# Attention: the row maxima kept in the rounded f32 type and turned by a product with an identity of that type

## The reference

```python
x = x + diff_attention(layernorm(x))      # two causal softmaxes per head, 8 heads of 2 x 16
x = x + experts_gelu(layernorm(x))        # shared MLP and top 2 of 8 experts
x = x + causal_attention(layernorm(x))    # 16 heads of 8
x = x + experts_gelu(layernorm(x))
x = x + single_head_attention(layernorm(x))
x = x + full_attention_and_experts(x)     # rmsnorm, 16 heads of 8, no mask; then top 2 of 8 experts, swiglu
x = x + gated_recurrence(x)
x = x + full_attention_and_experts(x)
```

```python
scores = einsum('bhqd,bhkd->bhqk', q, k) * scale     # masked in the causal ones
attn = softmax(scores, axis=-1)
out = einsum('bhqk,bhkd->bhqd', attn, v)
```

## Time and profile before

| | |
|---|---|
| time, median of 3 runs | 2595.62 us (2595.09 to 2595.83) |
| the profiled execution | 2601.83 us, span 2600.1 us |
| TensorE busy / weight loads | 2246.4 us (86%) / 1646.6 us (63%) |
| VectorE, ScalarE, GpSimd busy | 1761.2, 1597.1, 1179.9 us |
| mean granted TensorE clock | 0.94 |
| turning the maxima (L1687) | 520 products in 260 calls |

### The profile page before, as it was taken

One profiled execution on the slowest core, in us unless ns is written; L12 is line 12 of the kernel. 1 busy time (PEld: TensorE's weight loads), 2 busy tenths in 40 slices (PEclk: granted clock), 3 DMA queues, 4 the chain that ended last, 5 costly groups with the idle time before them and its releaser, 6 DMA issues. The chain is left out here.

```text
span 2600.1 us, 59924 instructions
## 1 busy us (share of the span) xinstructions
PE 2246.4 (86%) x19192; PEld 1646.6 (63%) x19192; DVE 1761.2 (68%) x4845; ACT 1597.1 (61%) x3559; POOL 1179.9 (45%) x1645
## 2 busy tenths in 40 slices
PE   5999998899699888999778888889676788887896
PEld 3666665699566655799665555589333455555695
DVE  5677777444478776543767888576777577887666
ACT  3666665367566665476548888444465368887344
POOL 3456665445244555455122354457333323454463
PEclk9999999899799998999879999899888989999998
DMA  8000000322200002122100000222200000001225
GB/s 312 24 4 12 12 12 12 99 60 71 81 2 6 16 17 87 44 70 77 47 5 2 10 17 17 74 66 83 76 0 7 4 2 3 17 17 35 75 81 137
DMA packets 133603, 116.54 MB, mean 45 GB/s; under 512 B 22903, under 2 KB 119685, under 8 KB 131264
## 3 DMA queue, kind: packets, MB, share of 16 engines
q1 hardware_dynamic: 116032, 78.17, 10.4%
q0 software_dynamic: 17280, 34.65, 4.1%
HBM read 58.22 MB, written 56.36 MB: 44 GB/s over the span
## 5 line engine op out<-in xcount | busy, mean ns | idle before, releaser
L1216 ACT ACTIVATE A_Pm<-A_t 128x768 f32<-128x768 f32 (+1 forms) x512 | 469.1, 916 | 152.3 <-PE A_t L1645 149.5
L372 POOL DMA_INDIRECT ybuf<-F_yo,F_idx x284 | 315.7, 1112 | 265.0 <-DVE F_yo L581 161.2
L1412 DVE TENSOR_REDUCE A_padm<-A_s 128x4 f32<-128x1024 f32 x264 | 322.6, 1222 | 55.9 <-PE A_s L1637 53.2
L224 POOL DMA_INDIRECT xbuf<-xs,dst x256 | 268.4, 1048 | 105.9 <-issue 60.4
L733 PE MATMUL F_hb<-F_xT,F_wt 128*128 128x128 f32 x2272 | 311.3, 281 | 3.0 <-issue 1.5
L1672 PE MATMUL A_ot<-A_Pm,A_V 128*32 128x256 f32 (+3 forms) x3640 | 295.5, 389 | 16.9 <-POOL A_Pm L1111 10.0
L1645 PE MATMUL A_t<-A_Q,A_K 32*128 32x256 f32 (+1 forms) x2560 | 304.9, 332 | 0.0
L1111 POOL TENSOR_SCALAR_AFFINE_SELECT A_Pm<-A_Pm 128x512 f32<-128x512 f32 x256 | 168.4, 658 | 292.7 <-ACT A_Pm L1216 291.0
L733 PEld LDWEIGHTS F_hb<-F_xT,F_wt 128*128 128x128 f32 x2272 | 281.0, 195 | 9.4 <-issue 3.2
L1637 PE MATMUL A_s<-A_K,A_Q 32*128 32x256 f32 (+1 forms) x1584 | 202.7, 332 | 66.3 <-DVE A_padm L1412 31.3
L745 PE MATMUL F_out<-F_WA,F_g 128*128 x1704 | 247.9, 282 | 4.7 <-DVE F_g L572 1.6
(11 more groups left out here) (426 smaller groups left out, 5064.9 us busy)
## 6 DMA issues: line engine op xcount, KB each, us to landing
F_xr<-xbuf SPq DMA_DIRECT2D x284, 68.0 KB, 1.8
xbuf<-A_zero SPq DMA_DIRECT2D x16, 1088.0 KB, 17.5
xs<-ybuf SPq DMA_DIRECT2D x32, 512.0 KB, 6.9
ybuf<-F_yo,F_idx POOLq DMA_INDIRECT x284
xbuf<-xs,dst POOLq DMA_INDIRECT x256, 2.4
F_WA<-in_L_ffn_ew SPq DMA_DIRECT2D x2, 2048.0 KB, 9.0
F_WA<-in_L_ffn_ew SPq DMA_DIRECT2D x16, 256.0 KB, 5.8
F_WA<-in_L_ffn_e_gate SPq DMA_DIRECT2D x2, 1024.0 KB, 5.7
```

Source lines behind the costliest of these rows:

```text
L224: pool.indirect_dma_start(out=G["XBUF"][:, :], out_offset=bass.IndirectOffsetOnAxis(ap=G["dst"][:, t, c:c + 1], axis=0), in_=G["xs"][c][:, ...
L372: pool.indirect_dma_start(out=YBUF[:, :], out_offset=bass.IndirectOffsetOnAxis(ap=idx[n][:, h:h + 1], axis=0), in_=yo[r][:, h, :], in_offs ...
L1216: act.activation(Pm[r][:, j:j + 2, :], tbank[:, :].rearrange("p (j k) -> p j k", j=2)[:, :, 0:PW], ACT.Exp, scale=SCALE).then_inc(t_free, 1)
L1412: last = dve.reduce_max(tops.rearrange("p t j -> p j t"), sbank[:, :].rearrange("p (j t k) -> p j t k", j=2, t=TPS), AX)
```

## The change

`padm` becomes F32R (its memsets write the same zeros), a copy `identr` of the identity in F32R is made once by VectorE in `init_globals`, and `turn_max` issues a plain product of `padm` with `identr` where it issued a transpose of `padm` with `ident`. Every instruction keeps its place on its engine; one cast is added on VectorE ahead of the first stage.

```diff
@@ sparse_constants
     G["Mrun"] = ctx.enter_context(nc.sbuf_tensor("Mrun", [P, E], BF16))
+    G["identr"] = ctx.enter_context(nc.sbuf_tensor("identr", [P, P], F32R))
@@ init_globals, vector
                 dve.tensor_copy(xs[c][:, :, D], C["ids"][:, c, :])
+            dve.tensor_copy(G["identr"][:, :], ident[:, :])
@@ attention_stage
-    padm = [sb(f"padm{k}", [P, TPS, QUAD, GR]) for k in range(2)]
+    padm = [sb(f"padm{k}", [P, TPS, QUAD, GR], F32R) for k in range(2)]
@@ attention_stage, gpsimd
-            pool.memset(padm[0][:, :, :, :], 0.0)
-            pool.memset(padm[1][:, :, :, :], 0.0).then_inc(p_set, 1)
+            pool.memset(padm[0][:, :, :, :].bitcast(F32), 0.0)
+            pool.memset(padm[1][:, :, :, :].bitcast(F32), 0.0).then_inc(p_set, 1)
@@ turn_max
                 for t in range(TPS):
-                    last = pe.transpose(mbank[:, t * P:(t + 1) * P], padm[r][:, t, :, :].rearrange("p r g -> p (r g)"), ident[:, :])
+                    last = pe.matmul(mbank[:, t * P:(t + 1) * P], padm[r][:, t, :, :].rearrange("p r g -> p (r g)"), G["identr"][:, :], start=True, stop=True)
                 last.then_inc(mt_full, 1)
```

## The result

The changed kernel takes **2604.45 us** (median of 20 executions, 2598.43 to 2610.64); the kernel before took 2596.95 us (20 executions, 2593.12 to 2603.27) on the same chip. The ratio is 1.0025, with a 95% interval of 1.0018 to 1.0031: **slower by 0.25%**. The forecast of 2594.9 us was wrong, and so was its range, which ended at 2601. The profiled execution took 2604.19 us (span 2602.5), which is at the median; that of before was 4.9 us over its own. So the two profiles are only 2.4 us apart and show too little of the loss; it must be read by stage.

A forecast was written before the change was run, and what follows sets the result against it. TensorE was taken as the bound in the first attention stage (421 of 429 us busy), with slack elsewhere. Terms 0.3 - 0.5 - 0.8 + 0.3 = -0.7 us took the median from 2595.62 to 2594.9 us; range 2588 to 2601 us.

The forecast's parts named there:

- The pair: Two turned products at the changed line: 0.45 us to the end, 0.38 to the next load, taken as +0.005 us each.
- Behind the logits: Pairs after the router's logits: next load at 0.37 us instead of 0.46; -0.5 us first stage, -0.8 us other stages.
- The second load waits: Rival: the pair's second load starts only after the first product's columns, 0.054 us a pair, +6.3 to +14.0 us; chance 0.06.
- the load is as short: Rival: the rounded load is as short as the transposed one, saving 0.11 us a pair, 2583 to 2588 us; chance 0.04.
- the rounded maxima cost VectorE: Rival: writing maxima in the rounded type costs 9 ns or more at 792 reductions, up to +7 us; chance 0.03.
- the 177 pairs of the other stages: Pairs outside the first stage, not behind logits: only 0.005 us at each of 52 VectorE waits counts, +0.3 us.
- The clock (slower): Rival: less TensorE streaming lowers its clock; 13 us more at the lower level loses 5.2 us, 2602 us; chance 0.03.
- The clock (faster): Rival: plain products release the clock earlier in the last three attention stages, up to 4.8 us each, 2580.5 at best; chance 0.05.

The follow-up runs named there:

- e2: Changed kernel with f32 transposes instead of products, keeping the rounded type, identity copy and cast; 0.9980 of the kernel before.
- e10: Repeat, in a later comparison, of the changed kernel with f32 transposes and the rounded type kept; 1.0001 of the kernel before.
- e6: Changed kernel with the product only in the two unmasked stages (fourth and fifth), f32 transposes in the masked ones; 1.0018 of the kernel before.
- e9: The changed kernel unaltered, run again in a later comparison; 1.0031 of the kernel before.
- e1: The changed kernel unaltered, run again in another comparison; 1.0020 of the kernel before.
- e11: Changed kernel with both products of each pair streaming 256 columns, the second half into an unread block; 1.0019 of the kernel before.
- e5: Changed kernel with the product only in the two masked stages, f32 transposes in the unmasked ones, all types kept; 1.0002 of the kernel before.
- e4: Kernel before plus two unused f32 identity products after the third group's turn in the second, fourth and fifth stage; 1.0007 of the kernel before.

## Why the prediction was wrong

- **The pair: right.** 0.44 us to its end and 0.37 to the next load, forecast within 0.01; the longer load and the shorter streaming cancel. Behind the logits 0.37 instead of 0.46, as the sum had it. "The second load waits", "the load is as short" and "the rounded maxima cost VectorE" did not happen: the loads are 189 ns, the reductions 1222 ns as before, and e2 and e10 clear the type. The first stage shows it in one number, 304.96 against 305.01 us over 48 pairs.
- **The step that failed** is the sum's entry for the 177 pairs of the other stages: "TensorE has slack behind them", and of the pair "Only the 0.005 us in the result counts". I took slack as free for time saved on TensorE. It is free for time on the path; but the saving of 0.108 us in each group came out of what the array streams, in stretches of which some 40% held no product at all, and the clock then fell after some of them. The entry was worth +0.3 us in the sum; the fourth and fifth stage lost 5.2 us in the first profile, 12.4 to 14.7 in e6 and e9.
- **The rival that happened** is "The clock (slower)", named and priced, with a chance of 0.03. The price of a us was good: "5.2 us would be lost after 13 us more at it", and the profile has 5.2 us for 13.6 us. That the length came out near 13 us too is luck: nothing in the prediction said how much longer the clock would be low, and later profiles have 30.6 and 40.8 us. The reason against it was poor: "the upper level held through the rest of the stage with 15% of TensorE's time idle" is a mean over 311 us. The stage's sparsest stretches have 1.95 us of products in 3.40, 43% without any, and are found by cutting the stage into short stretches. In the trace of before they stood open, one at 1453.30, with the clock at 1.00 and nothing to tell how near to a fall it was.
- **Size.** The rows give 0.30 to 0.38 us lost for each us at the lower level (e1 against e2 9.0 us for 30.6, e9 against e10 14.7 for 40.8, e6 against e5 12.4 for 34.0, the first comparison 5.2 for 13.6). The other executions agree roughly by their mean clock: e9's 0.9343 against e10's 0.9390 is 0.0047 x 2 x 2655 = 25 us more at half rate, which at 0.30 to 0.38 is an estimate of 7.5 to 9.5 us, and the medians are 9.8 us apart. The profile of e9 shows more than that because it is its slowest execution. In the first comparison only the changed kernel's profile and before's can be set side by side; of its 7.5 us, 5.2 are shown in them and the rest is not placed. The range was also tighter than its own sum: the bounds reached +6.8 us, which is 2602.4, and the range was said to end at 2601. The measured time lies over both.
- **"The clock (faster)"** did not happen. The stretches of the earlier trace rows are as they were, with the first eight turned products in 22.00 us at 0.71 and the next eight in 17.20 at 1.00. The Trainium skill's page TensorE: Matmul & The Clock Gate (Part 4: PE-mode transpose) says that transposes don't count as the array being busy in the same way as products; with them replaced by plain products the clock should then have held better. It held worse: 3, 6 and 9 falls with the products (the changed kernel, e1, e9) against none with f32 transposes (before, e2, e10), and none either with plain products of the transposes' streaming length (e11). So for these f32 transposes of 128 columns the measurement speaks against the page.
- **A page that pointed near it.** The idle times that frame the fall are waits for VectorE and ScalarE of 0.7 us each. The Trainium skill's page TensorE: Matmul & The Clock Gate (section A second HAM failure mode: psum-queue depth-cycling) tells of another kernel, where TensorE idles briefly between groups of products often enough for its clock to go back and forth, and throughput suffers by it while the median product looks healthy. The falls here look like that, and I had not weighed it. But the same idle times stand in the kernel before, whose clock held, so the page doesn't tell the two kernels apart.
- The advice against the change (the Trainium skill, Perfetto Trace Analysis, section Transposes: turn by a transpose) held in its outcome, by a mechanism that the page doesn't name: at this size the transpose costs the pair the same time, and keeps the array streaming twice as long.

## What to carry to other kernels

TensorE's clock follows its own work, so time saved on it in a stage with slack need not be worth zero: here it was worth less. Before shortening TensorE's work in a stage with slack, cut that stage into stretches of a few us, find the sparsest, and ask what the edit takes out of it; a mean over the stage hides it, and busy time by records can't see columns. Where such an edit is wanted, try it first where the engine is the bound (here the product in the masked stages alone, e5, neither gained nor lost: 1.0002, and no fall in the others), and when a result is in, compare the granted clock of each stage before anything else. One profile shows one execution; the mean clock over all of them says whether it is typical.

## What the hardware showed that I had not expected

- The same 30 records in the same 2.06 of 3.40 us were followed by 1.00 of the clock or by 0.50; the work differed by 0.108 us of streaming, and the changed kernel too kept the upper level after most stretches like it. In all seven profiles with products in the full stages of which one or both streamed 128 columns there was a fall (1 to 9); of the seven with transposes there, or with both products 256 wide, six had none, and e4 had four.
- Idle time that stands together is not enough for a fall: e2 and e10 have seven idle times of 1.35 to 1.39 us each, a stretch of 3.40 us with 1.54 and 1.58 us of products, and no fall; e4, with as many, had four.
- A pair of plain products in the rounded type reaches its next load after 0.37 us, like the pair of f32 transposes, and with 256 columns after 0.43: loads of 189 instead of 141 ns cancel what the shorter streaming saves.
- The 35 falls of all profiles lasted 3.4 or 6.8 us each. Of the 25 in the kernels with products and no fill or wide product (the changed kernel, e1, e6, e9), 19 began 0.95 to 1.4 us after the turned pair of a third group, in one sequence or another: a place in the order of work, met anew in each execution.
